# One expert number at a time: writing out the tile loops of the expert layer in a graph-network kernel

## The chip, the cores and the metric

The kernel runs on one core of one Trainium2 chip. The metric is the device time of one execution in microseconds (us), from launch to the last write. The core has a TensorE (PE, with its weight loads shown as PEld), a VectorE (DVE), a ScalarE (ACT), a GpSimd (POOL) and a SyncE (SP). Each engine takes its instructions from a queue of its own, in order, and engines wait for each other by semaphores. Register instructions (address arithmetic, loads of a number from memory into a register, branches) are carried out by the sequencer that hands the engine its work; the profile shows them with a q behind the engine, as PEldq, DVEq or ACTq.

## The reference

Two layers of a graph network over 6250 nodes of 256 features, each followed by a feed-forward part. The change touches only the feed-forward part of the first layer, a mixture of eight experts of which each node takes two:

```python
B, S, D, E, H, K = (4, 512, 256, 8, 512, 2)
gate_scores = x @ Wg + bg
_, idx = jax.lax.top_k(gate_scores, K)
mask = jax.nn.one_hot(idx, E, dtype=x.dtype).sum(axis=-2)
h = jax.nn.gelu(jnp.einsum('td,edh->teh', xf, W1) + b1[None], approximate=False)
y = jnp.einsum('teh,ehd->ted', h, W2) + b2[None]
out = jnp.einsum('ted,te->td', y, mf)
```

Everything else (edge gathers, two graph convolutions, two linear attentions, the gated mixture at the end) is the same in both kernels.

## The kernel before

The program is a row of phases with a barrier between them. The phase `route` picks two experts for each node and sorts the node-expert pairs by expert; `send_to_experts` writes the rows of each expert one after the other; `experts` does the products; `second_norm` collects them. In `experts` the sorted rows are cut into MT = 106 tiles of 128 rows, and all rows of a tile belong to one expert. Which expert that is depends on the data, so its number is in a table in on-chip memory (`tile_expert`, one number a tile), and each engine that needs it loads it into a register. With the number, an engine works out the address of the expert's weights or bias (`ds(e, 1)`).

For each tile `i`, with two buffers (`b = i % 2`):

- SP loads the tile's 128 rows (`load`, with a table and a register of its own).
- PE turns them (`turn_x`, two transposes, L2742), makes the hidden layer (`hidden`, 24 products of 128 columns, L2756) and the result (`result`, 12 products of 256 columns, L2769). Numbers are split in a high and a low half of 16 bits, three products for one.
- ACT takes the high part of the turned rows (`x_high_part`, L2673) and computes gelu in four instructions (`gelu`, L2682).
- DVE makes the low part (`x_split`, L2700), splits gelu's output (`g_split`, L2708 and L2710) and adds the bias to the result (`y_rows`, L2716), which POOL stores (L2665).

The work is laid out so that the queues overlap: for tile `i`, PE's queue has `hidden(i)`, `result(i - 2)`, `turn_x(i + 2)`; ACT's has `gelu(i)`, `x_high_part(i + 2)`; DVE's has `y_rows(i - 2)`, `g_split(i)`, `x_split(i + 2)`.

What sets the order is written out by hand in `turns`. Two tiles are a `body`; three bodies, so six tiles, are one pass of a hardware loop (`Fori`, L2630), and there are 17 passes. The first two tiles and the last two stand outside of the loop. At the top of each pass `experts_of` (L2622) loads all the numbers that the pass needs with one instruction: eight on PE (tiles `i - 2` to `i + 5`), six on ACT, six on DVE. Behind the load stand two instructions for each number, which put it in its own register and test its range. Waits inside the loop compare a semaphore with a register, since the count depends on the pass; the lines L2740, L2747, L2750 and L2764 are such waits on PE, and some need a register instruction to work out the count. Only PE, ACT and DVE use `turns`; SP and POOL have their own loops, which stay.

Of the kernel before, what the change touches and what calls it, by code (L numbers as in the profile page):

```python
# [118 lines left out]
MT = (2 * NP + EXPERTS * (P - 1)) // P  # L119
# [2479 lines left out]
def experts(c):  # L2599
# [20 lines left out]
    def experts_of(engine, tile, n):  # L2620

        _, regs = nc.values_load_multi_w_load_instructions(c.tile_expert[0:1, ds(tile, n)], engines=[engine.engine],  # L2622
                                                           min_val=0, max_val=EXPERTS - 1)
        return list(regs)

    def turns(engine, body, back, n):


        body(0, [None] * back + experts_of(engine, 0, n - back) if n > back else None, True, False)
        with engine.Fori(0, (MT // 2 - 2) // 3) as r:  # L2630
            q = r * 3 + 1
            e = experts_of(engine, q * 2 - back, 4 + n)
            for j in range(3):
                body(q + j, e[2 * j:2 * j + n], False, False)
        q = MT // 2 - 1
        body(q, experts_of(engine, q * 2 - back, n), False, True)
    assert (MT // 2 - 2) % 3 == 0

    with nc.Block() as block:

        @block.sync
        def _(sp):
            sp.dma_start(b2.rearrange("p e d -> p (e d)"),
                         c.inp["L0_ffn_b2"].rearrange("e d -> (e d)").unsqueeze(0).partition_broadcast(P)).then_inc(loaded, 16)

            def load(i, b):
                row = sp.value_load(c.tile_row[0:1, ds(i, 1)], min_val=0, max_val=EXPERTS * REGION - P)
                sp.dma_start(x[:, b, :], c.slot_x[ds(row, P), :]).then_inc(x_ready[b], 16)

            for b in range(2):  # L2650
                load(b, b)
            with sp.Fori(0, MT // 2 - 1) as q:
                for b in range(2):

                    sp.wait_ge(turned, q * 2 + b + 1)
                    load(q * 2 + 2 + b, b)
            sp.wait_ge(loaded, c.constants.at(16))

        @block.gpsimd
        def _(gp):  # L2660
            with gp.Fori(0, MT // 2) as q:
                for b in range(2):
                    gp.wait_ge(y_out, q * 2 + b + 1)
                    gp.sem_inc(c.passed, 1)
                    gp.dma_start(c.slot_y[ds((q * 2 + b) * P, P), :], y[:, b, :]).then_inc(stored[b], 16)  # L2665
            for b in range(2):
                gp.wait_ge(stored[b], 16 * (MT // 2))

        @block.scalar
        def _(a):  # L2670
            def x_high_part(i, b):
                a.wait_ge(turned, i + 1)
                a.activation(xT[:, b, 0, :], c.psum[:, b, 0:D], ACT.Copy, scale=XS).then_inc(x_high, 1)  # L2673

            def gelu(i, b, first, e):
                a.wait_ge(h_ready, i + 1)
                if not first:

                    a.wait_ge(g_low, i - 1)
                at = COLUMNS_AT["L0_ffn_b1"][0]  # L2680
                for m in range(HM):
                    ins = a.activation(g[:, b, m * P:(m + 1) * P], c.psum[:, 2 + b, m * P:(m + 1) * P], ACT.Gelu,  # L2682
                                       bias=c.cols[:, ds(e * HM + (at + m), 1)], scale=1.0 / (XS * WS))
                ins.then_inc(g_ready, 1)

            x_high_part(0, 0)
            x_high_part(1, 1)

            def body(q, e, first, last):
                for b in range(2):  # L2690
                    gelu(q * 2 + b, b, first, e[b])
                    if not last:
                        x_high_part(q * 2 + b + 2, b)
            turns(a, body, 0, 2)

        @block.vector
        def _(v):
            def x_split(i, b):
                v.wait_ge(x_high, i + 1)
                v.scalar_tensor_tensor(xT[:, b, 1, :], c.psum[:, b, 0:D], XS, xT[:, b, 0, :], ALU.mult, ALU.subtract  # L2700
                                       ).then_inc(x_low, 1)

            def g_split(i, b, first):
                v.wait_ge(g_ready, i + 1)
                if not first:

                    v.wait_ge(y_ready, i - 1)
                v.tensor_scalar(gT[:, b, 0, :], g[:, b, :], XS, None, ALU.mult).then_inc(g_high, 1)  # L2708
                v.wait_ge(g_high, i + 1)
                v.scalar_tensor_tensor(gT[:, b, 1, :], g[:, b, :], XS, gT[:, b, 0, :], ALU.mult, ALU.subtract  # L2710
                                       ).then_inc(g_low, 1)

            def y_rows(i, b, pair, e):
                v.wait_ge(y_ready, i + 1)
                v.wait_ge(stored[b], pair * 16)
                v.scalar_tensor_tensor(y[:, b, :], c.psum[:, 4 + b, 0:D], 1.0 / (XS * WS),  # L2716
                                       b2[:, ds(e, 1), :].rearrange("p e d -> p (e d)"), ALU.mult, ALU.add
                                       ).then_inc(y_out, 1)

            v.wait_ge(loaded, c.constants.at(16))  # L2720
            x_split(0, 0)
            x_split(1, 1)

            def body(q, e, first, last):
                for b in range(2):
                    i = q * 2 + b
                    if not first:
                        y_rows(i - 2, b, q - 1, e[b])
                    g_split(i, b, first)
                    if not last:  # L2730
                        x_split(i + 2, b)
            turns(v, body, 2, 2)
            e = experts_of(v, MT - 2, 2)
            for b in range(2):
                y_rows(MT - 2 + b, b, MT // 2 - 1, e[b])

        @block.tensor
        def _(pe):
            def turn_x(i, b, pair):
                pe.wait_ge(x_ready[b], (pair + 1) * 16)  # L2740
                for k in range(2):
                    last = pe.transpose(c.psum[:, b, k * P:(k + 1) * P], x[:, b, k * P:(k + 1) * P], c.ident[:])  # L2742
                last.then_inc(turned, 1)

            def hidden(i, b, first, e):

                pe.wait_ge(x_low, i + 1)  # L2747
                if not first:

                    pe.wait_ge(g_ready, i - 1)  # L2750
                for m in range(HM):
                    n = 0
                    for k in range(2):
                        for wp, xp in PARTS:
                            n += 1
                            last = pe.matmul(c.psum[:, 2 + b, m * P:(m + 1) * P],  # L2756
                                             c.w1_16[:, ds(e, 1), k, wp, m * P:(m + 1) * P].rearrange("p e n -> p (e n)"),
                                             xT[:, b, xp, k * P:(k + 1) * P], start=(n == 1), stop=(n == 6))
                last.then_inc(h_ready, 1)

            def result(i, b, pair, e):
                pe.wait_ge(g_low, i + 1)

                pe.wait_ge(y_out, pair * 2)  # L2764
                n = 0
                for m in range(HM):
                    for wp, gp in PARTS:
                        n += 1
                        last = pe.matmul(c.psum[:, 4 + b, 0:D], gT[:, b, gp, m * P:(m + 1) * P],  # L2769
                                         c.w2_16[:, ds(e, 1), m, wp, :].rearrange("p e n -> p (e n)"),  # L2770
                                         start=(n == 1), stop=(n == 3 * HM))
                last.then_inc(y_ready, 1)

            turn_x(0, 0, 0)
            turn_x(1, 1, 0)

            def body(q, e, first, last):
                for b in range(2):
                    i = q * 2 + b
                    hidden(i, b, first, e[2 + b])  # L2780
                    if not first:
                        result(i - 2, b, q - 1, e[b])
                    if not last:
                        turn_x(i + 2, b, q + 1)
            turns(pe, body, 2, 4)
            e = experts_of(pe, MT - 2, 2)
            for b in range(2):
                result(MT - 2 + b, b, MT // 2 - 1, e[b])
    c.constants.end(16)


# [1246 lines left out]
```

## Time and profile before

| | us |
|---|---|
| median of 3 executions | 4109.37 |
| lowest, highest | 4106.85, 4113.02 |
| the profiled execution | 4104.44 |
| its span, from first to last instruction | 4102.8 |
| PE busy in the span | 2951.5 (72%) |
| DVE busy | 2469.6 (60%) |
| ACT busy | 1236.8 (30%) |
| mean granted share of TensorE's full clock | 0.841 |

The profiled execution lies 4.9 us below the median. The phase `experts` fills about 440 us of it, from 2088 us to 2530 us after the start; the phases ahead of it and behind it are parted from it by barriers, so what it gains or loses moves the end by as much. Read the profile of this phase in two ways: by the engines' own work (the timeline), and by what their sequencers do between it (rows with a q).

### The profile page before, as it was taken

The page shows a single profiled execution, that of the slowest core. Times are in us where ns is not written, and L with a number is a line of the kernel's source. Part 1 is how long each engine was busy: PE and PEld are TensorE (multiplying, and loading weights), DVE is VectorE, ACT ScalarE, POOL GpSimd, SP SyncE. Part 2 cuts the span into 40 slices and gives each one's busy share as a digit, 9 for nine tenths or more (in the row PEclk, how much of TensorE's full clock was granted, in tenths as well). Part 3 has the DMA queues.
Part 4 walks back from the last instruction along what each step waited for, and adds up shares of the span by engine and source line. Part 5 has one row for each costly group of instructions (what it writes and reads, how often), then busy time and mean ns, then how long its engine had stood idle before and what let it go on. Part 6 is the DMA issues. An engine that isn't in the chain of part 4 may idle for free. (4 is left out here: it accounts for less than half of the span.)

```text
span 4102.8 us, 67269 instructions
## 1 busy us (share of the span) xinstructions
PE 2951.5 (72%) x20826; PEld 2101.5 (51%) x20827; DVE 2469.6 (60%) x7438; ACT 1236.8 (30%) x2741; POOL 1585.3 (39%) x1664
## 2 busy tenths in 40 slices
PE   2541788886988888483048885149999996998798
PEld 2440455553664555273047774126776774666444
DVE  6956888773444443466124444669887773678454
ACT  1202122331421001031123332136554441433554
POOL 1010777771027777321721112656555442333000
PEclk9655689998989999786579997559999998898899
DMA  4103444442035554354421112653333225011000
GB/s 136 77 29 120 128 144 135 159 158 75 23 123 159 160 159 143 112 174 160 143 83 62 66 64 81 209 189 107 99 99 89 82 81 173 29 42 37 27 23 27
DMA packets 242287, 429.53 MB, mean 105 GB/s; under 512 B 34308, under 2 KB 181303, under 8 KB 236825
## 3 DMA queue, kind: packets, MB, share of 16 engines
q0 software_dynamic: 71904, 196.05, 16.0%
q1 hardware_dynamic: 155552, 175.03, 13.0%
q10 hardware_dynamic: 14620, 55.77, 3.7%
q8 instruction: 116, 1.90, 0.2%
q14 instruction: 95, 0.78, 0.1%
HBM read 313.04 MB, written 113.68 MB: 104 GB/s over the span
## 5 line engine op out<-in xcount | busy, mean ns | idle before, releaser
L1132 POOL DMA_INDIRECT scr<-xn_table,src_i x392 | 373.5, 953 | 340.3 <-PE psum L977 221.1
L1132 POOL DMA_INDIRECT scr<-h_table,src_i x392 | 371.5, 948 | 326.5 <-issue 324.4
L1132 POOL DMA_INDIRECT xnT<-xn_table,src_i x392 | 375.2, 957 | 257.5 <-issue 222.2
L977 PE MATMUL psum<-scr 128*128 128x128 f16 (+1 forms) x3136 | 318.5, 259 | 89.0 <-issue 82.1
L977 PEld LDWEIGHTS psum<-scr 128*128 128x128 f16 (+1 forms) x3136 | 297.4, 153 | 131.3 <-issue 99.2
L759 ACT ACTIVATE scr<-scr,agg 128x128 f16<-128x128 f16 x710 | 252.2, 395 | 80.3 <-DVE scr L742 73.7
L2756 PE MATMUL psum<-scr,xnT 128*128 128x128 f16 x2544 | 198.8, 234 | 64.2 <-issue 58.6
L984 DVE SCALAR_TENSOR_TENSOR agg<-psum,agg 128x256 f32 (+1 forms) x196 | 95.1, 485 | 234.5 <-PE psum L971 215.0
L740 DVE TENSOR_SCALAR scr<-iota,agg 128x128 f16<-128x128 bf16 x710 | 223.9, 318 | 9.0 <-PEq L3044 9.0
L789 PE MATMUL psum<-xnT,agg 128*128 128x512 f16 x637 | 223.9, 389 | 0.6 <-DVE agg L726 0.6
L2756 PEld LDWEIGHTS psum<-scr,xnT 128*128 x2544 | 177.6, 104 | 82.4 <-issue 68.9
L3939 PE MATMUL psum<-scr 128*128 128x512 f16 (+2 forms) x1197 | 206.2, 325 | 16.6 <-ACT scr L3877 9.8
L2665 POOL DMA_DIRECT2D expert_results<-scr x106 | 57.4, 541 | 398.5 <-DVE scr L2716 398.5
L614 DVE TENSOR_SCALAR scr<-iota,scr 128x128 f16<-128x128 bf16 x710 | 188.5, 274 | 35.9 <-PE psum L665 29.5
L641 ACT ACTIVATE agg<-psum 128x392 f16<-128x392 f32 x208 | 103.3, 497 | 339.7 <-PE psum L665 339.6
L615 DVE TENSOR_SCALAR scr<-expert_scores,scr 128x98 f16<-128x98 f16 (+3 forms) x710 | 199.8, 291 | 0.0
L742 DVE TENSOR_SCALAR scr<-expert_scores,agg 128x98 f16<-128x98 f16 (+3 forms) x710 | 194.4, 276 | 0.0
L665 PE MATMUL psum<-scr 128*128 128x98 f16 (+3 forms) x710 | 133.8, 256 | 80.8 <-DVE scr L615 70.8
L2716 DVE SCALAR_TENSOR_TENSOR scr<-psum,scr 128x256 f32<-128x256 f32 x106 | 45.0, 424 | 239.3 <-PE psum L2769 239.3
L2682 ACT ACTIVATE scr<-psum,feature_columns 128x128 f32<-128x128 f32 x424 | 121.3, 369 | 219.2 <-PE psum L2756 204.0
L2742 PE MATMUL psum<-ident,scr 128*128 128x128 f32 x212 | 42.4, 284 | 195.7 <-DMA scr<-expert_rows 195.7
L791 PE MATMUL psum<-xnT,scr 128*128 128x256 f16 x637 | 177.4, 279 | 0.0
(499 smaller groups left out, 7063.8 us busy)
## 6 DMA issues: line engine op xcount, KB each, us to landing
adjacency_table<-agg ACTq DMA_DIRECT2D x13, 1568.0 KB, 6.3
scr<-adjacency_table ACTq DMA_DIRECT2D x13, 1568.0 KB, 7.5
scr<-expert_rows SPq DMA_DIRECT2D x106, 128.0 KB, 2.0
expert_results<-scr POOLq DMA_DIRECT2D x106, 128.0 KB, 2.1
scr<-xnT_table SPq DMA_DIRECT2D x98, 128.0 KB, 3.1
xnT<-xnT_table SPq DMA_DIRECT2D x2, 5376.0 KB, 22.6
agg<-in_L_ffn_W SPq DMA_DIRECT2D x16, 512.0 KB, 9.7
x_table<-scr SPq DMA_DIRECT2D x14, 512.0 KB, 3.1
```

The costliest lines, as they stand in the source:

```text
L614: v.tensor_scalar(self.place_hot[:, u, :], c.iota16[:], self.lists[:, 1, r:r + 1], None, ALU.is_equal)
L615: v.tensor_scalar(self.code_hot[:, u, 0:wide], c.iota_wide[:, 0:wide], self.lists[:, 0, r:r + 1], None, ALU.is_equal).then_inc(self.rows_h ...
L665: pe.matmul(c.psum[:, 5 + t % 2, at:at + wide * HI], self.place_hot[:, n % self.ring, :], self.code_hot[:, n % self.ring, 0:wide * HI], st ...
L740: v.tensor_scalar(self.place_hot[:, u, 0, :], c.iota16[:], self.list_at("low", r), self.list_at("weight", r), ALU.is_equal, ALU.mult)
L742: v.tensor_scalar(self.code_hot[:, u, 0:wide], c.iota_wide[:, 0:wide], self.list_at("code", r), None, ALU.is_equal).then_inc(self.rows_hot, 1)
L759: a.activation(self.place_hot[:, u, 1, :], self.place_hot[:, u, 0, :], ACT.Copy, scale=self.list_at("ratio", r)).then_inc(self.rows_low, 1)
L789: pe.matmul(c.psum[:, 7, :], self.adjacency[:, tile % 2, h, :], self.x16[:, h, :], start=(h == 0), stop=False, skip_group_check=True)
L791: last = pe.matmul(c.psum[:, 7, 0:D], self.low[:, tile % 2, h, :], self.x16[:, h, 0:D], start=False, stop=(h == HI - 1), skip_group_check= ...
L977: last = pe.matmul(bank[b][:, s, :], lhs, hot[:, hot_b, t, :], start=(t == 0 and n == 0), stop=(t == CT - 1 and n == pieces - 1))
L1132: g.indirect_dma_start(out=rows[:, u, t, :], out_offset=None, in_=table, in_offset=bass.IndirectOffsetOnAxis(ap=index(t), axis=0)).then_in ...
L2756: last = pe.matmul(c.psum[:, 2 + b, m * P:(m + 1) * P], c.w1_16[:, ds(e, 1), k, wp, m * P:(m + 1) * P].rearrange("p e n -> p (e n)"), xT[: ...
L3939: last = pe.matmul(out, weights(wp), moving(xp), start=(first and i == 0), stop=(k_last and i == 2))
```

## The change

`turns` is removed, with the loops over passes on PE, ACT and DVE. Each of the three now has the work of all 106 tiles written out, in the same order as before. In place of one load of eight (or six) numbers at the top of a pass there is one load of one number for each tile (`one_of`): on PE between `hidden(i)` and `result(i - 2)`, on ACT between `gelu(i)` and `x_high_part(i + 2)`, on DVE behind `x_split(i + 2)`. PE keeps the numbers of three tiles in registers, since `result` comes two tiles after `hidden`. All waits now compare a semaphore with a constant.

```diff
-    def turns(engine, body, back, n):
-
-
-        body(0, [None] * back + experts_of(engine, 0, n - back) if n > back else None, True, False)
-        with engine.Fori(0, (MT // 2 - 2) // 3) as r:
-            q = r * 3 + 1
-            e = experts_of(engine, q * 2 - back, 4 + n)
-            for j in range(3):
-                body(q + j, e[2 * j:2 * j + n], False, False)
-        q = MT // 2 - 1
-        body(q, experts_of(engine, q * 2 - back, n), False, True)
-    assert (MT // 2 - 2) % 3 == 0
+    def one_of(engine, tile):
+
+        return experts_of(engine, tile, 1)[0]
...
+            e = one_of(a, 0)
+            for i in range(MT):
+                gelu(i, i % 2, i < 2, e)
+                if i + 1 < MT:
+                    e = one_of(a, i + 1)
+                if i + 2 < MT:
+                    x_high_part(i + 2, i % 2)
...
+            e = one_of(v, 0)
+            for i in range(MT + 2):
+                if i >= 2:
+                    y_rows(i - 2, i % 2, i // 2 - 1, e)
+                if i < MT:
+                    g_split(i, i % 2, i < 2)
+                if i + 2 < MT:
+                    x_split(i + 2, i % 2)
+                if 2 <= i <= MT:
+                    e = one_of(v, i - 1)
...
-            def body(q, e, first, last):
-                for b in range(2):
-                    i = q * 2 + b
-                    hidden(i, b, first, e[2 + b])
-                    if not first:
-                        result(i - 2, b, q - 1, e[b])
-                    if not last:
-                        turn_x(i + 2, b, q + 1)
-            turns(pe, body, 2, 4)
-            e = experts_of(pe, MT - 2, 2)
-            for b in range(2):
-                result(MT - 2 + b, b, MT // 2 - 1, e[b])
+            e = {0: one_of(pe, 0)}
+            for i in range(MT + 2):
+                if i < MT:
+                    hidden(i, i % 2, i < 2, e[i])
+                if i + 1 < MT:
+                    e[i + 1] = one_of(pe, i + 1)
+                if i >= 2:
+                    result(i - 2, i % 2, i // 2 - 1, e.pop(i - 2))
+                if i + 2 < MT:
+                    turn_x(i + 2, i % 2, i // 2 + 1)
```

How this moves instructions on PE, at the top of a loop pass. Before, from the last transposes of the tile ahead (L2742) to the first products of `hidden` (L2756); `ISA` and `REGISTER_ALU` are register instructions:

```order
L2742 MATMUL psum<-ident,scr 128x128 x2
L2630 UNCONDITIONAL_BRANCH
L2630 ISA
L2622 REGISTER_ALU
L2622 TENSOR_LOAD expert_of_tile
L2622 ISA x16
L2747 REGISTER_ALU
L2750 REGISTER_ALU
L2756 ISA
L2756 MATMUL psum<-scr,xnT 128x128 x2
```

The same engine after the change, in the middle of any tile, from the end of `hidden` (now L2745) to the start of `result` (now L2758):

```order
L2745 ISA
L2745 MATMUL psum<-scr,xnT 128x128
L2622 TENSOR_LOAD expert_of_tile
L2622 ISA x2
L2758 REGISTER_ALU
L2758 MATMUL psum<-scr 128x256 x2
```

The load with its sixteen register instructions, once in six tiles, has become a load with two, once in each tile, and it stands in front of `result`.

Between two tiles of a pass on PE, before, from the end of `result` (L2769) over `turn_x` to `hidden`:

```order
L2769 MATMUL psum<-scr 128x256
L2740 ISA
L2742 MATMUL psum<-ident,scr 128x128 x2
L2747 REGISTER_ALU
L2756 ISA
L2756 MATMUL psum<-scr,xnT 128x128 x2
```

and after:

```order
L2758 MATMUL psum<-scr 128x256
L2731 MATMUL psum<-ident,scr 128x128 x2
L2745 ISA
L2745 MATMUL psum<-scr,xnT 128x128 x2
```

The two register instructions that worked out counts to wait for (L2740, L2747) are gone; the ones that work out the weights' addresses (L2745, L2758) stay.

## Rows read from the trace of the kernel before

**Rows 1.** Timeline of PE over a loop top: start, length, idle before.

```profile
2139.62 1.47 PE L2769 MATMUL psum<-scr 128*128 x12
...
2142.89 1.47 PE L2769 MATMUL psum<-scr 128*128 x12
2144.20 0.38 PE L2742 MATMUL psum<-ident,scr 128*128 128x128 f32 x2
2144.42 1.86 PE L2756 MATMUL psum<-scr,xnT 128*128 128x128 f16 x24
2146.27 1.47 PE L2769 MATMUL psum<-scr 128*128 x12
2147.58 0.38 PE L2742 MATMUL psum<-ident,scr 128*128 128x128 f32 x2
2150.97 2.69 PE L2756 MATMUL psum<-scr,xnT 128*128 128x128 f16 x24 [3.00 <-issue]
```

**Rows 2.** Sequencer at L2756, four tiles (two in pass one): ns, first and last start.

```profile
L2756 PEldq FUSED_REGOPS  x16: 46/46/46, 2144.0 to 2146.0; - x16
...
L2756 PEldq FUSED_REGOPS  x16: 46/46/46, 2108.3 to 2110.4; - x16
...
L2756 PEldq FUSED_REGOPS  x16: 46/46/46, 2115.3 to 2117.4; - x16
...
L2756 PEldq FUSED_REGOPS  x16: 46/46/46, 2134.0 to 2135.9; - x16
```

**Rows 3.** Sequencer at L2769 in the same tile.

```profile
L2769 PEldq ALU_OP  x8: 32/32/32, 2146.2 to 2147.0; - x8
```

**Rows 4.** Sequencer at L2630 and L2622, the loop top at 2147 us.

```profile
L2630 PEldq ALU_OP  x1: 32/32/32, 2147.1 to 2147.1; - x1
L2630 PEldq COMPARE_BRANCH  x1: 207/207/207, 2147.2 to 2147.2; - x1
...
L2622 PEldq FUSED_REGOPS  x8: 146/146/151, 2148.4 to 2150.4; - x8
L2622 PEldq SEQ_ASSERT  x8: 18/18/18, 2148.6 to 2150.6; - x8
...
L2622 PEldq TENSOR_LOAD <-expert_of_tile x1: 599/599/599, 2147.7 to 2147.7; - x1
```

**Rows 5.** Other loads: PE in pass two, first tiles, last tiles; one on DVE.

```profile
L2622 PEldq TENSOR_LOAD <-expert_of_tile x1: 1942/1942/1942, 2122.6 to 2122.6; - x1
...
L2622 PEldq TENSOR_LOAD <-expert_of_tile x1: 551/551/551, 2091.9 to 2091.9; - x1
...
L2622 PEldq TENSOR_LOAD <-expert_of_tile x1: 1019/1019/1019, 2516.0 to 2516.0; - x1
...
L2622 DVEq TENSOR_LOAD <-expert_of_tile x1: 531/531/531, 2517.6 to 2517.6; - x1
```

**Rows 6.** Loads of a single number: L1101 on PE, L2647 on SP.

```profile
L1101 PEldq TENSOR_LOAD <-flag_i x3: 306/314/1078, 413.9 to 2735.8; - x3
...
L2647 SPq TENSOR_LOAD <-first_row_of_tile x106: 263/270/512, 2086.7 to 2510.1; - x106
```

**Rows 7.** Windows, one for each of the first five passes, then low and high clock.

```profile
core 0: us, PE busy (x) PEld busy (x) DVE busy (x) ACT busy (x) POOL busy (x), PEclk, DMA share, GB/s
2097.90:2122.60 24.70, 21.56 (x230) 18.29 (x228) 11.73 (x26) 11.14 (x38) 2.82 (x5) 0.93 0.20 65
2122.60:2147.70 25.10, 20.70 (x231) 18.38 (x228) 10.70 (x24) 9.17 (x30) 3.24 (x6) 0.93 0.20 63
2147.70:2171.40 23.70, 20.70 (x230) 18.40 (x229) 10.71 (x24) 9.17 (x30) 3.24 (x6) 0.93 0.20 66
2171.40:2197.20 25.80, 21.48 (x230) 18.98 (x229) 10.70 (x24) 9.17 (x30) 3.24 (x6) 0.87 0.19 61
2197.20:2221.30 24.10, 21.13 (x231) 18.18 (x229) 10.71 (x24) 9.17 (x30) 3.24 (x6) 0.93 0.19 65
...
2151.10:2154.50 3.40, 3.40 (x30) 3.09 (x29) 0.00 (x0) 0.61 (x3) 0.00 (x0) 0.51 0.00 0
2154.50:2174.90 20.40, 17.18 (x201) 15.21 (x198) 10.71 (x24) 8.55 (x29) 3.24 (x6) 1.00 0.24 77
```

**Rows 8.** PE's register instructions for waits, the whole phase.

```profile
L2747 PEldq ALU_OP  x68: 32/32/36, 2100.9 to 2512.5; - x68
L2747 PEldq FUSED_REGOPS  x34: 42/44/46, 2108.1 to 2509.1; - x34
...
L2740 PEldq FUSED_REGOPS  x51: 42/42/42, 2104.3 to 2512.4; - x51
```

**Rows 9.** Instruction fetch: DMA queues in the first pass; then in the other sixteen.

```profile
q1 hardware_dynamic: 1008, 0.92, 12.6%
q0 software_dynamic: 240, 0.66, 7.0%
q8 instruction: 2, 0.03, 0.5%
q14 instruction: 1, 0.01, 0.1%
...
q1 hardware_dynamic: 13680, 12.46, 11.1%
q0 software_dynamic: 4560, 12.46, 8.1%
```

**Rows 10.** Timeline of DVE, third tile's `x_split`; PE's first loop product.

```profile
2099.78 0.42 DVE L2700 SCALAR_TENSOR_TENSOR scr<-psum,scr 128x256 f16<-128x256 f32 x1
...
2101.20 2.18 PE L2756 MATMUL psum<-scr,xnT 128*128 128x128 f16 x24 [3.08 <-DVE scr L2700]
```

**Rows 11.** Waits inside one pass (2130.6 to 2147.5 us): total, times, longest.

```profile
DVE scr L2716 <- PE psum L2769: 12.8, 5, 7.3
ACT scr L2682 <- PE psum L2756: 6.6, 5, 1.4
ACT scr L2673 <- PE psum L2742: 2.0, 5, 0.6
```

More of the change, by code:

```diff
@@ L2687, in _ @@
             x_high_part(1, 1)
-            def body(q, e, first, last):
-                for b in range(2):
-                    gelu(q * 2 + b, b, first, e[b])
-                    if not last:
-                        x_high_part(q * 2 + b + 2, b)
-            turns(a, body, 0, 2)
+            e = one_of(a, 0)
[5 more added lines that the diff above has]
+                    x_high_part(i + 2, i % 2)
         @block.vector
@@ L2722, in _ @@
             x_split(1, 1)
-            def body(q, e, first, last):
-                for b in range(2):
-                    i = q * 2 + b
-                    if not first:
[L2728 to L2735, printed above, removed]
+            e = one_of(v, 0)
[8 more added lines that the diff above has]
+                    e = one_of(v, i - 1)
         @block.tensor
@@ L2775, in _ @@
             turn_x(1, 1, 0)
-            def body(q, e, first, last):
-                for b in range(2):
-                    i = q * 2 + b
-                    hidden(i, b, first, e[2 + b])
-                    if not first:
-                        result(i - 2, b, q - 1, e[b])
-                    if not last:
-                        turn_x(i + 2, b, q + 1)
-            turns(pe, body, 2, 4)
-            e = experts_of(pe, MT - 2, 2)
-            for b in range(2):
-                result(MT - 2 + b, b, MT // 2 - 1, e[b])
+            e = {0: one_of(pe, 0)}
[8 more added lines that the diff above has]
+                    turn_x(i + 2, i % 2, i // 2 + 1)
     c.constants.end(16)
```

## The prediction

> **What bounds the kernel now.** I read the timeline of PE in the experts phase first. Inside a pass the products stand back to back [rows 1]: `result` starts at 2139.62, 2142.89 and 2146.27, so a tile takes 3.27 to 3.38 us, 3.33 on average. At the top of a pass PE is idle for 3.00 us, put down to "issue". The waits inside a pass [rows 11] say that DVE and ACT wait for PE, and no row has PE waiting for them. So PE's side sets the pace; the question is which part of it.
>
> It is the sequencer, not the array. In one tile the 16 register instructions ahead of the `hidden` products start from 2144.0 to 2146.0 us [rows 2], which is 15 steps of 0.13 us; the 24 products take 1.86 us [rows 1], about as long as the steps. The eight ahead of the `result` products start from 2146.2 to 2147.0 [rows 3], 0.11 us a step. Together that is 2.0 + 0.13 + 0.9 us, and with the transposes and waits (0.3) it is the whole 3.33 us. The array itself needs less: 12 `result` products start within 1.31 us (2146.27 to 2147.58, the next group's start [rows 1]), `hidden` has the same number of columns, so 1.3 again, and two transposes 0.2: 2.9 us. So each register instruction that PE's sequencer gains or loses in a tile lengthens or shortens the tile by its full time, up to about 0.45 us of shortening, where the array takes over.
>
> The loop top [rows 4] on that sequencer: the loop's own instruction at 2147.1, the branch (0.21 us), the load at 2147.7 for 0.60 us, then eight pairs of register instructions whose first starts run from 2148.4 to 2150.4, about 0.28 us a pair, of which 0.146 and 0.018 are the instructions; that leaves a gap of 0.06 behind each. The next tile's instructions begin at about 2150.7: 3.6 us for six tiles. Every second pass the load takes 1.94 us [rows 5], and the top then costs 4.9. The passes confirm it [rows 7]: six tiles at 3.33 are 20.0, plus 3.6 is 23.6 (measured 23.7 and 24.1), plus 4.9 is 24.9 (measured 25.1 and 25.8). Over the phase: from 2097.9 to 2516.0 (the load behind the last pass [rows 5]) there are 17 passes in 418.1 us, 4.10 us a tile. The rest, some 0.3 us a pass, goes with the clock: right behind the loop top it is at the lower of its two levels (1.2 GHz) for 3.4 us, then at 2.4 GHz for 20.4 us [rows 7], and `hidden` takes 2.69 us there in place of 1.86 [rows 1].
>
> **The change part by part**, all on PE's sequencer, for one of the 102 tiles that the loop held.
>
> The load of one number. No row of this phase has one on PE, but the loads of two, four and (slow kind) eight numbers took 0.551, 1.019 and 1.942 us [rows 5], a line of 0.233 a number over 0.085, which gives 0.32 for one. The single loads elsewhere on PE took 0.306 and 0.314 us, one of three 1.078; 106 single loads on SP in this very phase took 0.270 in the median, 0.512 at most [rows 6]. I take 0.31. With the gap of 0.06 behind it and one pair of register instructions (0.28) it holds the queue for 0.65 us a tile. The bounds are 0.27 (SP) and 0.60 (the eight-number load [rows 4]), so 0.61 to 0.94; the far end of 1.08 would make 1.42.
>
> The waits' counts. L2747 (102 times) and L2740 (51 times) vanish [rows 8]: 153 instructions of 32 to 46 ns, with the 0.06 gap about 0.10 us each, 15.3 us or 0.15 a tile. L2750 and L2764 each keep one instruction in a tile: nothing.
>
> The loop top. All of it goes: 3.6 or 4.9 us a pass, 0.70 a tile, and the low clock that follows it, 0.3 us a pass. What is late next is nothing new: the same sequencer.
>
> The code itself. After the change all of it runs once and has to be fetched. A pass run again fetches nothing: there are instruction packets in the first pass and none in the sixteen others [rows 9]. The first pass is thus the sample for code that runs once: 24.7 us, where other passes with the short load took 23.7 and 24.1 [rows 7], so 0.8 us more on average, 0.13 a tile. Part of that is the wait for DVE at its start [rows 10]. I take 0.10; the bounds are zero and 0.17 (24.7 less 23.7, over six).
>
> The Trainium skill has a rule for each of the two disputed terms. DMA: Bandwidth & Descriptors (Latency and other measured facts) puts the floor of a register load at about 600 ns and says that the compiler groups four to spread it, which speaks against this change; here 0.31 and 0.27 us for single loads [rows 6] stand below that floor. Runtime: NRT & Kernel Launch (Instruction fetch mechanics) says that straight code is fetched ahead and the cost is mostly hidden; that would make the code term near zero, where the first pass shows 0.1 a tile [rows 7].
>
> A new tile: 3.33 - 0.15 + 0.65 + 0.10 = 3.93 us. 102 of them are 400.9. They can start no earlier than before allows in one place: the third tile's `hidden` needs DVE's `x_split`, done at 2100.2 [rows 10], 2.3 us after the load at 2097.9 that used to cover it. So 403.2 in place of 418.1: 14.9 us less. In the last tiles, loads of four numbers (1.02 + 0.06 + 4 x 0.28 = 2.2) and of two (1.2) give way to a single 0.65; 2.7 less, of which I count 2, since some is covered by products still in the queue. Sum: 17 us less. The profiled execution would go from 4104.4 to 4087.4; the median of the runs stands 4.9 above it, so 4092.
>
> ACT and DVE get a load a tile too: on DVE two numbers took 0.531 us [rows 5], no more than on PE, so some 0.3 + 0.3 us beside 10.7 us of work in six tiles (1.8 a tile) [rows 7], and on ACT the same beside 1.5. Both stay at about 2.5 us in a tile of 3.9, and DVE waits 12.8 us, ACT 8.6, inside one pass [rows 11]. I cost them at nothing. What they feed has slack too: `result(i)` comes two tiles behind `hidden(i)`, and `x_split` is wanted one tile later. If that cover were gone, their 0.6 us would come on top, 60 us in all.
>
> **Rivals.** First, *the fetch is hidden*: the 0.8 us of the first pass is the wait for DVE and the cold clock alone. Then a tile takes 3.83 us and the time is 4092 - 10 = 4082. Against it: the 16 register instructions of a tile spread over 2.1 us in the first pass, over 1.9 to 2.0 in the second [rows 2], though nothing is waited for between them. The rule on fetching named above would have it so.
>
> Second, *the load costs what a load of eight costs*, 0.60 us, whatever its size: 0.29 more a tile, 29.6 us, so 4122, slower than before. The rule on the load's floor named above would make the same. The break-even is a load of 0.31 + 17/102 = 0.48 us, and from 0.56 on the change is slower by more than can be measured. Against it are 106 rows on SP and two of three on PE; for it, the one of 1.078 and that three engines and SP now load at scattered times.
>
> Third, *the clock falls in the tile*. PE's array now has a gap of about half a microsecond in each tile in place of one long one in six. At 1.2 GHz the array needs 5.8 us for a tile (twice 2.9) and would be the bound over 3.93. Stretches of 3.4 us as now, once in 24 us, cost 1.1 us each, 18 us in all: 4110, no change; half the phase at the low level would cost 60. Against it: the array's gap is 0.2 to 0.6 us long, and the clock held at 2.4 GHz through the six tiles of a pass [rows 7].
>
> Fourth, *fetching straight code stalls more than in the first pass* (0.2 to 0.3 us a tile, as 102 tiles have no earlier stock to run on), or ACT or DVE hold PE up a little: 4102 to 4112, no change.
>
> The change doing something other than it says is excluded by the order: one load and two register instructions stand in every tile.
>
> **How the numbers follow.** About 0.2% (8 us) is what a measurement of this kernel can tell from no change. My sum (4084 to 4100 with the load at 0.27 to 0.33 and the code term at 0.05 to 0.17): 0.54. Hidden fetch, 4076 to 4084: 0.20. Clock in short stretches or more stalls, 4101 to 4114: 0.16. Load at its floor or a fallen clock, 4118 and more: 0.10. The first two are faster, with a small share at the edge: 0.73. Same: 0.18, slower: 0.09. The range leaves out the far load and the fallen clock and the last few of the others: 4076 to 4108.
>
> **What would show it.** Each step has its row in the profile after. The load on PE: a duration of about 0.31 us, 106 times. The tile: starts of `result` 3.9 us apart with no gap of 3 us; the idle time before `result` should be about 0.4 us each, put down to issue. The code term: register instructions of `hidden` spread over 2.0 to 2.1 us rather than 1.9, and instruction packets all through the phase. The clock: 1.00 in the phase, from 0.93 and 0.87. The phase from the first loop product to the last transposes about 400 us. The prediction is wrong if loads take over 0.5 us, if the clock drops below 0.9, or if the idle time before `hidden` or `result` is put down to ACT or DVE.

## The result and the profile after

| | before | after |
|---|---|---|
| median of 6 executions, us | 4109.09 | 4089.3 |
| ratio, 95% interval | | 0.9955, 0.9942 to 0.9967 |
| span of the profiled execution, us | 4102.8 | 4087.0 |
| first transpose to last product of the experts phase, us | 438.0 | 421.9 |

The change makes the kernel 20 us faster by the medians, and the interval leaves no doubt that it is faster, though by less than 0.6% (0.48% by the medians). In the two profiled executions the span is 15.8 us shorter, and the experts phase by itself is 16.1 us shorter; the phases around it scatter by 2 to 3 us in both directions. So some 16 us is what the traces show of the change, and the few us that the medians have beyond that are not placed.

The timeline of PE in the middle of the phase (start, length, idle before) answers to [rows 1]:

```profile
2286.98 1.47 PE L2758 MATMUL psum<-scr 128*128 x12 [0.63 <-issue]
2288.29 0.38 PE L2731 MATMUL psum<-ident,scr 128*128 128x128 f32 x2
2288.51 1.74 PE L2745 MATMUL psum<-scr,xnT 128*128 128x128 f16 x24
2290.88 1.47 PE L2758 MATMUL psum<-scr 128*128 x12 [0.64 <-issue]
2292.19 0.38 PE L2731 MATMUL psum<-ident,scr 128*128 128x128 f32 x2
2292.41 1.79 PE L2745 MATMUL psum<-scr,xnT 128*128 128x128 f16 x24
2294.90 1.47 PE L2758 MATMUL psum<-scr 128*128 x12 [0.70 <-issue]
```

There is no stall of 3 us any more; a stall of 0.6 to 0.7 us stands in front of each `result`. From one `result` to the next it is 3.90 and 4.02 us.

The sequencer rows of L2622 over the phase, with ns as min/median/max (compare [rows 4, 5, 6]):

```profile
L2622 PEldq TENSOR_LOAD <-expert_of_tile x106: 296/301/317, 2094.4 to 2506.8; - x106
L2622 PEldq FUSED_REGOPS  x106: 151/151/156, 2094.8 to 2507.2; - x106
L2622 PEldq SEQ_ASSERT  x106: 18/18/18, 2095.0 to 2507.4; - x106
L2622 ACTq TENSOR_LOAD <-expert_of_tile x106: 274/450/545, 2095.3 to 2507.5; - x106
...
L2622 DVEq TENSOR_LOAD <-expert_of_tile x106: 300/303/366, 2095.7 to 2514.9; - x106
```

The load of one number takes 0.30 us on PE, 106 times with hardly any spread. Two windows, the first over 400 us of the phase (busy time of each engine, then the granted clock), and the queues that carry instructions between 2122 and 2515 us:

```profile
2105.70:2505.70 400.00, 332.07 (x3862) 291.12 (x3863) 180.95 (x406) 155.42 (x509) 54.59 (x101) 1.00 0.21 68
...
q8 instruction: 41, 0.67, 0.7%
q14 instruction: 18, 0.15, 0.1%
```

The clock is at its full level (2.4 GHz) all through this window, where the passes of before had 0.93 and 0.87 [rows 7], and instruction packets come in it, where the loop had none after its first pass [rows 9].

Since the sequencer's instructions are all in the trace, a tile can be cut in four by their starts. These are means of the trace's starts, over steady tiles of before (three in each pass, away from the loop top) and over 92 tiles after:

| part of a tile on PE's sequencer, us | before | after |
|---|---|---|
| first to last of the 16 register instructions of `hidden` | 1.926 | 1.961 |
| from there to the first of `result`, with the load | 0.233 | 0.906 |
| first to last of the 8 of `result` | 0.796 | 0.838 |
| from there to the next `hidden`, with the counts | 0.396 | 0.236 |
| sum | 3.352 | 3.941 |

The load is 0.67, the counts -0.16, and the two stretches of products 0.08 longer. A tile of before that bears its share of the loop top takes 4.07 us (over 100 tiles), 0.72 more than a steady one: 0.66 for the loop top and 0.06 for the two or three slower tiles behind it, where the clock is low. So the change gains 0.13 us a tile: 0.72 + 0.16 - 0.67 - 0.08.

### The profile page after: what moved, and what is told of

It reads as the page before. It is cut to its first block and busy times, and to the rows that moved or that the text cites. A ratio compares the mean times of both kernels' runs of the same rounds, so it can differ in the third digit from the quotient of the medians.

```text
span 4087.0 us, 66648 instructions
## 1 busy us (share of the span) xinstructions
PE 2920.7 (71%) x20826; PEld 2073.3 (51%) x20826; DVE 2470.7 (60%) x7437; ACT 1238.2 (30%) x2740; POOL 1584.0 (39%) x1664
## 5 line engine op out<-in xcount | busy, mean ns | idle before, releaser
L2758 PE MATMUL psum<-scr 128*128 x1272 | 155.9, 272 | 69.8 <-issue 60.4
L2745 PE MATMUL psum<-scr,xnT 128*128 128x128 f16 x2544 | 186.6, 222 | 2.0 <-DVE scr L2691 1.7
L2745 PEld LDWEIGHTS psum<-scr,xnT 128*128 x2544 | 165.7, 98 | 20.1 <-issue 3.7
```

Source lines behind the costliest of these rows:

```text
L2745: last = pe.matmul(c.psum[:, 2 + b, m * P:(m + 1) * P], c.w1_16[:, ds(e, 1), k, wp, m * P:(m + 1) * P].rearrange("p e n -> p (e n)"), xT[: ...
```

## The experiments

All ratios are against the kernel before on the same chip. The kernel before took between 4105.2 and 4110.6 us in these sets and the changed kernel was not run again beside them, so a difference from the changed kernel's 4089.3 us, or between two experiments of different sets, is uncertain by some us. The length of the experts phase in the profiled execution (first transpose to last product) scatters less, since only the experts phase differs between these kernels, and is given with each time: 438.0 us before, 421.9 after. One view serves for all: the window from 2120 to 2440 us, well inside the phase, where the count of POOL's stores (the fifth pair of numbers) is the number of tiles done in 320 us, and the clock stands behind it. Before and after:

```profile
2120.00:2440.00 320.00, 271.60 (x2952) 239.10 (x2951) 138.56 (x311) 118.68 (x389) 42.12 (x78) 0.91 0.19 64
```

```profile
2120.00:2440.00 320.00, 265.37 (x3087) 232.48 (x3085) 145.61 (x326) 123.82 (x405) 44.20 (x82) 1.00 0.21 69
```

78 tiles against 82.

### Written out, but with the loads in groups as before

```diff
-                if i + 1 < MT:
-                    e[i + 1] = one_of(pe, i + 1)
+                if i % 6 == 2 or i == MT:
+                    count = 2 if i == MT else 4 if i == MT - 2 else 8
+                    e = dict(zip(range(i - 2, i - 2 + count), experts_of(pe, i - 2, count)))
```

and the same on ACT and DVE with six.

> One part alone: the loops are written out as in the change, but each engine still loads eight (six) numbers at once, at the same six-tile spacing as before. Theory (the gain comes from the loop's own instructions and the worked-out counts, and splitting the loads is about neutral on PE's sequencer): a tile without load 3.28 us, six of them 19.7, a load top of 1.27 on average + 0.06 + 8 x 0.28 = 3.6, cold clock behind it 0.3, so 23.6 a group in place of 24.6: 17 us less than before, 4092, within 5 us of the changed kernel. Rival (the gain comes from breaking the 3 us stall up into small ones): the stall and the low clock are still there, so this stays within 5 us of before, 4104 to 4109.

Measured: 4086.9 us, ratio 0.9945 (0.9927 to 0.9963), no different from the changed kernel by the medians. The phase takes 424.2 us, 13.8 less than before and 2.4 more than after the change. The stall is still there, and so is the low clock behind it:

```profile
2309.22 0.38 PE L2731 MATMUL psum<-ident,scr 128*128 128x128 f32 x2
2313.34 2.74 PE L2745 MATMUL psum<-scr,xnT 128*128 128x128 f16 x24 [3.73 <-issue]
```

```profile
2120.00:2440.00 320.00, 278.36 (x3047) 242.43 (x3048) 141.88 (x319) 121.63 (x400) 43.04 (x80) 0.93 0.21 68
```

So 13.8 of the 16.1 us in the phase come with writing the loops out. Splitting the loads, the half of the change that looks like the remedy for the stall, moves the stall into the tiles and is worth about 2 us: six loads with their tests hold the sequencer for 6 x 0.67 = 4.0 us, one grouped load lengthens its tile by 3.5 on average, and the low clock behind it costs another 0.6 (by the trace's starts, the two tiles behind the stall take 0.09 and 0.51 us more than the others).

### PE's loads doubled

```diff
+                    one_of(pe, i + 1)
                     e[i + 1] = one_of(pe, i + 1)
```

> The changed kernel with each of PE's single loads but the first done twice (105 more, one unused). Theory (PE's sequencer sets the pace, a load with its two register instructions holds it for 0.65 us): 105 x 0.65 = 68 us more than the changed kernel, 4157, tile 4.60 us, clock possibly below 1.00. Rival (the array or another engine shares the bound, so part of a load is hidden): under 50 us more.

Measured: 4169.1 us, ratio 1.0145 (1.0124 to 1.0167), 80 us more than the changed kernel where 68 was expected; the phase takes 499.5 us, 77.6 more. Nothing of the second load is hidden, which is what a sequencer-bound tile asks for; the rival is out. The excess is in the loads themselves: the 105 added ones bring 43.5 us, 0.41 each, since 64 of PE's 211 loads take between 0.33 and 0.55 us. Which ones, the end of the next section says.

```profile
L2622 PEldq TENSOR_LOAD <-expert_of_tile x211: 295/305/554, 2088.3 to 2578.2; - x106
...
2306.68 1.47 PE L2758 MATMUL psum<-scr 128*128 x12 [1.45 <-issue]
```

```profile
2120.00:2440.00 320.00, 221.97 (x2590) 195.03 (x2588) 121.62 (x272) 103.67 (x340) 36.69 (x68) 1.00 0.18 57
```

PE idles 1.3 to 1.6 us in every tile here, and the clock stays at 1.00.

### ACT's and DVE's loads doubled

```diff
+                    one_of(a, i + 1)
                     e = one_of(a, i + 1)
...
+                    one_of(v, i - 1)
                     e = one_of(v, i - 1)
```

> The changed kernel with ACT's and DVE's single loads but the first done twice. Theory (both have over 1 us of slack in a tile): no change against the changed kernel, 4089, within 4 us. Rival (the twelve waits of the result products for DVE's g_split in the profile after mean that DVE or ACT is nearly as late as PE): 20 us more or over, and PE's waits for DVE grow.

Measured: 4087.8 us, ratio 0.9946 (0.9926 to 0.9967), and a phase of 421.8 us against 421.9: nothing. This was the question of a row in the profile after that I had not expected, waits of PE for DVE's `g_split` (L2701), here of the changed kernel and then of this one (total, times, longest):

```profile
PE psum L2758 <- issue: 60.4, 91, 0.8
...
PE psum L2758 <- DVE scr L2701: 8.6, 12, 0.8
```

```profile
PE psum L2760 <- issue: 58.5, 90, 0.7
PE psum L2760 <- DVE scr L2702: 8.8, 13, 0.8
```

The waits for DVE are as long as the idle times put down to issue (at most 0.8 us) and don't grow when DVE gets 0.6 us more to do. Where that load takes longer (PE's loads doubled) or stands elsewhere (the grouped loads above), no wait of `result` for `g_split` is left in the profile. So the load on PE's own sequencer ends them, and DVE is named because its signal is the last that the profile sees.

### PE loads four at a time

```diff
-                if i + 1 < MT:
-                    e[i + 1] = one_of(pe, i + 1)
+                if i + 1 < MT and (i + 1) % 4 == 0 and i + 1 not in e:
+                    count = min(4, MT - i - 1)
+                    e.update(zip(range(i + 1, i + 1 + count), experts_of(pe, i + 1, count)))
```

> The changed kernel, but PE alone loads four numbers with one instruction every four tiles, starting at table places that are multiples of four. Theory (the load's time goes by how the numbers lie: eight from such a place took 0.60, so four take 0.30): 0.30 + 0.06 + 4 x 0.28 = 1.48 us for four tiles in place of 2.64, 0.29 a tile, 30 us less than the changed kernel: 4060. The array idles 1.3 us once in four tiles; should that let the clock fall, some 10 us of it are lost. Rival (the load's time is linear in the numbers, 1.02 for four): 2.2 in place of 2.64, 11 us less, 4078.

Measured: 4062.0 us, ratio 0.9888 (0.9869 to 0.9908), 27 us less than the changed kernel. The phase takes 393.1 us, 28.8 less.

```profile
L2622 PEldq TENSOR_LOAD <-expert_of_tile x27: 327/332/543, 2092.4 to 2472.2; - x27
...
2298.23 1.54 PE L2758 MATMUL psum<-scr 128*128 x12 [1.51 <-issue]
```

```profile
2120.00:2440.00 320.00, 285.15 (x3323) 250.47 (x3321) 156.70 (x351) 132.67 (x436) 47.49 (x88) 1.00 0.22 74
```

Four numbers cost one load of 0.33 us, hardly more than one number, and the clock is unharmed by the 1.5 us stall. It has to be a full four: the longest row, 0.543 us, is the last group, of the two numbers at place 104, which is a multiple of four too.

### The same groups, two places later

```diff
-                if i + 1 < MT and (i + 1) % 4 == 0 and i + 1 not in e:
+                if i + 1 < MT and (i + 1) % 4 == 2 and i + 1 not in e:
```

> As the kernel with groups of four, but the groups start two places later in the table (2, 6, 10). Theory (where the group starts decides): the load takes 1.02 us in place of 0.30, 0.18 a tile, 18 us more than with groups at multiples of four: 4078. Rival (only the count of numbers decides): the same time as the kernel with groups of four.

Measured: 4092.1 us, ratio 0.9958 (0.9941 to 0.9975), 30 us more than the other groups where 18 was expected. The phases differ by 28.5 us (421.6 against 393.1).

```profile
L2622 PEldq TENSOR_LOAD <-expert_of_tile x27: 553/1208/1268, 2091.8 to 2491.8; - x27
...
2304.04 2.31 PE L2758 MATMUL psum<-scr 128*128 x12 [2.38 <-issue]
```

```profile
2120.00:2440.00 320.00, 271.92 (x3080) 241.80 (x3077) 144.69 (x325) 123.71 (x406) 43.71 (x81) 0.93 0.21 68
```

The place decides: the load takes 1.21 us and not 0.33 (I had 1.02 for it, from the one such load of [rows 5]). 26 times 0.88 is 23 us (22 by the sum of the rows). What is left goes with the clock: behind the stall of 2.38 us above, the next 12 products take 2.31 us in place of 1.47, and the window's clock is 0.93. Not each stall of this length has it behind it (after the one that ends at 2320.0 us they take 1.47): 8 of 26 do. In the whole phase the clock stands low for 59 us, against 5 in the kernel with the other groups and 76 in the kernel before.

### No range test

```diff
-                                                           min_val=0, max_val=EXPERTS - 1)
+                                                           min_val=0, max_val=EXPERTS - 1,
+                                                           skip_runtime_bounds_check_because="route writes 0 to 7 alone")
```

> The changed kernel without the range test behind each expert number (on PE, ACT and DVE), so a load is one instruction and not three. Theory: two register instructions with their gaps, 0.28 us, less in each tile on PE: 29 us less than the changed kernel, 4060, tile 3.66. Rival (the load's latency overlaps with what follows, and the first user of the register waits instead): less than 15 us.

Measured: 4057.6 us, ratio 0.9874 (0.9857 to 0.9890), 32 us less than the changed kernel where 29 was expected. The phase takes 391.7 us, 30.2 less.

```profile
L2622 PEldq TENSOR_LOAD <-expert_of_tile x106: 296/300/315, 2092.8 to 2475.4; - x106
```

```profile
2120.00:2440.00 320.00, 287.44 (x3336) 251.47 (x3334) 157.04 (x352) 134.19 (x440) 47.49 (x88) 1.00 0.23 74
```

The two small register instructions behind each number, 0.15 and 0.02 us in the profile, cost nearly as much as the load.

### Both

> Both: PE loads four numbers at once at multiples of four, and no engine tests the range. Theory: 0.36 us for four tiles, 0.09 a tile in place of 0.66: 58 us less than the changed kernel, 4031, tile 3.37 us, clock 1.00. Rival (the array, at 2.9 us a tile, or DVE takes over first): a tile of 3.5 or more, 4045 or more.

Measured: 4025.5 us, ratio 0.9793 (0.9776 to 0.9809), 64 us less than the changed kernel and 85 less than the kernel before, which took 4110.6 on that chip. The phase takes 363.2 us, 58.6 less than after the change, where 58 was expected. It is the fastest of all.

```profile
2294.88 1.47 PE L2759 MATMUL psum<-scr 128*128 x12 [0.38 <-issue]
2296.19 0.38 PE L2732 MATMUL psum<-ident,scr 128*128 128x128 f32 x2
2296.41 1.76 PE L2746 MATMUL psum<-scr,xnT 128*128 128x128 f16 x24
2298.15 1.47 PE L2759 MATMUL psum<-scr 128*128 x12
```

```profile
2120.00:2440.00 320.00, 310.33 (x3614) 272.72 (x3613) 169.63 (x380) 144.68 (x476) 51.25 (x95) 1.00 0.24 80
```

A tile takes 3.37 us over the phase, as reckoned; `hidden` still takes 1.76 us, so it is still paced by its 16 register instructions and not by the array.

### What fetching costs: a loop of six tiles and one of thirty-four

The term for code that runs once was only read off a spread, so two kernels take it alone. Both keep the hardware loop, with the same instructions in a tile; only the length of the body differs.

```diff
+    BODIES = 3
...
+        with engine.Fori(0, (MT // 2 - 2) // BODIES) as r:
+            for j in range(BODIES):
+                body(r * BODIES + 1 + j, False, False)
...
+                    hidden(i, b, first, one_of(pe, i))
+                    if not first:
+                        result(i - 2, b, q - 1, one_of(pe, i - 2))
```

and BODIES = 17 in the other.

> The loops are kept (17 passes of six tiles, waits against registers, as before), but every number is loaded alone, and on PE twice a tile (once for hidden, once for result, since registers don't live on into the next pass). Theory: steady tile of before 3.35 us, two loads 1.32, two more register instructions for the load's place in the table 0.25, loop top 0.6 in six tiles: 5.0 us a tile against 4.10 before, 95 us more, 4204; from the second pass on no instruction packets; clock 1.00, since no gap is over 2 us. It is the partner of the loop of thirty-four.

> As the loop of six, but 3 passes of 34 tiles: instruction for instruction the same tile, only the body is so long that it has to be fetched in each pass. Theory (fetching costs PE's sequencer 0.08 us a tile, read from the trace of the changed kernel as 0.035 in hidden and 0.042 in result): 8 us more from fetching, 14 loop tops of 0.6 us less, so the same time within 3 us; the register instructions of hidden spread over 0.03 to 0.04 us more, those of result 0.04 more, and instruction packets come all through the phase. Rival (fetching is hidden, the spread has another cause): the spreads are the same in both and this kernel is 9 us faster.

Measured: 4206.5 us, ratio 1.0252 (1.0235 to 1.0269), and 4214.2 us, ratio 1.0263 (1.0245 to 1.0280). The first is 2.5 us from its forecast time; against its own set of the kernel before (4105.2) it is 101 us more where 95 was expected, and its phase, 536.7 us, is 98.7 longer. Its clock stood at 1.00 with idle times of 1.0 us at most in the loop; whether 2 us is a limit, as the text before the run takes it to be, no run here shows. Of the second, the spreads are as the theory has them: in the trace's starts the 16 register instructions of `hidden` take 1.929 us in the short loop and 1.985 in the long one, the 8 of `result` 0.880 and 0.907, together 0.083 us a tile. Instruction packets between 2150 and 2610 us: none on q8 in the short loop, in the long one

```profile
q8 instruction: 41, 0.67, 0.6%
```

But the whole is slower where I had expected no difference: 7.6 us by the medians, with runs that overlap (4204.0 to 4211.5 against 4207.3 to 4215.0), and 9.7 us in the phase. One thing was missing in my sum. The branches at the loop's end, the short loop first:

```profile
L2633 PEldq COMPARE_BRANCH  x17: 76/208/208, 2130.6 to 2614.4; - x17
```

```profile
L2633 PEldq COMPARE_BRANCH  x3: 79/3347/3387, 2272.9 to 2624.5; - x3
```

A branch back over six tiles takes 0.21 us; one back over thirty-four takes 3.35 to 3.39, and instruction packets move in that time. These are the queues from 2272.9 to 2276.3 us, during the first of them:

```profile
q8 instruction: 1, 0.02, 1.8%
q14 instruction: 2, 0.02, 1.7%
```

That fits code that has to be fetched before PE can go on. A low clock follows, 15 us of it in the phase against 5 in the short loop. Twice 3.15 us is 6.3. With 8.5 for fetching, less 6 for fourteen loop tops (0.43 us each in the short loop's trace, where 0.6 was expected), that makes 8.8 of the 9.7.

## Why the prediction was right

The time was forecast at 4092.0 and measured at 4089.3, inside the 4084 to 4100 of the likeliest case; the profiled execution's time at 4087.4, measured 4088.7. The gain of 17 us was nearly all put in the experts phase, which gave 16.1. By its own steps:

- **What bounds the kernel.** That PE's sequencer sets the pace was right, and the doubled loads show it: the added loads lengthen the phase by 77.6 us on PE and by nothing on ACT and DVE.
- **The load.** 0.31 us forecast, 0.301 measured; with what follows it 0.65 forecast, 0.67 measured. The rival of a 0.60 us load is out. The line drawn through the loads of two, four and eight numbers came near by luck: it makes 1.02 for any four, and four from a multiple of four take 0.33. The single loads elsewhere were the better ground. The Trainium skill's floor of about 600 ns for a register load (DMA: Bandwidth & Descriptors, Latency and other measured facts) doesn't hold here, where single loads take 0.30 us. Its remark that the compiler unrolls by four to spread that cost points the right way: one load for four tiles gained 27 us.
- **The counts.** 0.15 a tile forecast, 0.16 measured.
- **The code.** 0.10 a tile forecast, 0.077 measured against steady tiles of before, 0.083 between the two loops. The 0.10 was a choice between 0 and 0.17, not a sum, so part of the nearness is luck. The rival that fetching is hidden falls, though by little: it was for 0, and the truth is nearer to my value than to that. Its time, 4082, lies only 7 us from the measured one; the spreads decide against it, not the time.
- **The tile.** 3.93 forecast, 3.94 measured: 0.02 too little each for the load and the steady tile stand against 0.01 too little taken off for the counts and 0.02 too much for the code. Each error is small, and they nearly cancel.
- **The clock.** 1.00 as forecast; the rival of a clock that falls in the tile is out, and the doubled loads show that stalls of twice that length would not have made it fall. The low clock behind the old loop top costs 0.37 us a pass in the trace's starts, where 0.3 was put: it stood low for 76 of the phase's 438 us and still cost only some 6, since the array is not the bound.
- **The idle time before `result`** was put at 0.4 us and is 0.6 to 0.7. That is about the whole of the 0.67 that the load holds the sequencer, so hardly any products can have been left in the queue at the end of `hidden`. As the array is not the bound, nothing hangs on it.
- **A sign of being wrong that showed.** The prediction was to be wrong if idle time before `result` was put down to ACT or DVE, and 12 such waits are put down to DVE's `g_split`. With DVE's loads doubled they are 13 and the time is the same, so the sign misled and the step it stood for, that DVE has slack, holds.
- **What it left unsaid.** The sum was right, but it doesn't say which half of the change earns it. The written-out kernel with grouped loads does. Against it the change trades the grouped load and its low clock (3.5 + 0.6 us in six tiles, 0.69 a tile) for single loads (0.67 a tile), which is nearly even. What writing out alone earns is 0.12 a tile. The counts give 0.16 and the loop's own instructions 0.08 (the loop top lengthened its tile by 3.98 us on average, the grouped load alone by 3.53). Fetching takes back 0.08, and the low clock 0.04, since it costs 0.6 us in six tiles there in place of 0.37.

Why do some single loads take more than 0.33 us, most of ACT's in the changed kernel and 64 of PE's where they are doubled? The traces tell which ones do. I take the single loads of expert numbers on PE, ACT and DVE in all kernels that have them, 3071 in all, and the packets of tile rows on the queues q0 and q1. No load took over 0.323 us with no such packet under way; the 655 longer ones all ran beside some. In the changed kernel ACT's load runs beside them in 103 of 106 tiles. In the loop of six tiles it stands ahead of `gelu`, beside them once, and its time falls:

```profile
L2622 ACTq TENSOR_LOAD <-expert_of_tile x106: 273/278/288, 2093.3 to 2618.2; - x106
```

Two engines that load at once don't explain it: with ACT's and DVE's loads doubled, 100 loads of DVE overlap one of PE, and neither kind takes over 0.32 us. Not all loads beside packets are slow (some take 0.27 us), and what in the transfers delays them stays open. No run changed the transfers alone.

## What to carry to other kernels

Where the products are short and their addresses are in registers, look at the sequencer's rows before the array's: a tile's time can be the sum of its register instructions, and then each costs its duration plus a gap of 0.06 us, however small it looks. Judge a stall by what it does to that sum, not by its length: one stall of 3.6 us with its low clock and six of 0.67 cost nearly the same. Load register numbers in full groups of four from places that are multiples of four, see whether their range could be tested once where they are made (no run here did that; one left the test out and gained 32 us), and keep a loop's body short enough that its branch back needs no fetch, or write it out.

## What the runs showed of the hardware

- A load of numbers into registers on PE takes 0.30 us for one, 0.33 for four at a multiple of four, 0.60 for eight; from two places further on it takes 1.21 for four (1.02 in the one such load before) and 1.94 for eight. Two numbers take 0.55 from a multiple of four.
- Single loads took 0.27 to 0.32 us with no transfer of rows under way, and up to 0.56 beside one.
- Idle times of 1.3 to 1.6 us in every tile left TensorE's clock at 2.4 GHz; of 26 of 2.2 to 2.5 us, once in four tiles, 8 had 1.2 GHz behind them.
- PE ran six tiles again with a branch of 0.21 us and no instruction packets; a body of thirty-four tiles was fetched anew in each pass, and the branch back took 3.4 us. Straight code cost 0.08 us in a tile of some hundred instructions.
